# A fused attention and mixture-of-experts kernel: the down product in plain fp32, and fewer waits between scattered adds

## The chip, the cores and the metric

The kernel runs on one core of a Trainium2 chip. The metric is the device time of one execution in microseconds (us), given as the median of several runs. The engines of the core are named as the profile names them: PE (TensorE matmuls; PEld its weight loads), DVE (VectorE), ACT (ScalarE), POOL (GpSimd) and SP (SyncE, which only starts transfers here). Each runs its own instructions in order and waits on semaphores for the others.

## The reference, cut to what matters

Two transformer layers follow each other on x of 32 x 256 x 128 fp32. Each is an attention (16 heads of width 8; kind A over 256 positions with a relative bias, kind B over the batch) and then the same feed-forward layer: one shared expert for every token, and two of seven routed experts, chosen by a router and weighted.

```python
def _expert(h, g, u, d):
    return jnp.einsum('...i,hi->...h', jax.nn.silu(h @ g.T) * (h @ u.T), d)
...
shared_out = _expert(x, sg, su, sd)          # inner width 352
logits = x @ wr.T + rb
probs = jax.nn.softmax(logits, axis=-1)
scores, idx = jax.lax.top_k(probs, 2)
scores = scores / scores.sum(axis=-1, keepdims=True)
...
for e in range(7):
    out = out + w[..., e:e + 1] * _expert(x, rg[e], ru[e], rd[e])
...
x = x + attn_a(layernorm(x)); x = x + ffn(layernorm(x))
x = x + attn_b(layernorm(x)); x = x + ffn(layernorm(x))
```

## The kernel before

**Stages.** After a setup there are four stages: passes A, blocks A, passes B, blocks B. A pass handles 512 tokens: their attention, the router, the shared expert, and a scatter of each token's row to the regions of its two experts in a buffer in DRAM (`sent`, 8 indirect DMAs of POOL, step `place`). Passes overlap: the attention of one pass is interleaved with the expert part of the pass before. There are 16 passes of each kind.

**The planner.** The order of a pass's steps on each engine is not written by hand. `order` merges the attention steps and the expert steps of an engine from lists of needs (`needs_attention`, `needs_experts`) and modelled costs (`WORK`); of the steps that can start earliest it takes the one with the longest chain behind it (kind A) or that of the part further behind (kind B). In the order that it gives for kind B, PE's steps `down1`, `down2` and `end0` of the expert part stand after `bturn` and `bout`, the last attention steps, and are followed by `turn1`, `qk`, `v` and `spread` of the next pass. On POOL the steps stand as `tally`, `cut0`, `place`, `cut1`, `cut2`. On DVE `end0` stands after the last part of `norm2`.

**Blocks.** A block is 512 rows of one routed expert. The number of blocks is fixed, NB = 38 in each stage; a table made from the counts says where each block's rows lie and which expert's weights it takes. Blocks past the last expert are void: they read a spare region, and all add into the same dummy rows. For each block:
- SP loads the rows `xs` (a ring of 4 buffers; the load of block b waits until the adds of block b-4 have landed), then the gate and up weights `w_gu`, then the down weights `w_dn` (rings of 2).
- PE turns the rows (`turn_x`, four transposes into bank T). The turned rows are split into a high part in fp32r and the rest (`xbh`, `xbl`), and each product is three fp32r matmuls: high x high, high x low, low x high (`product`).
- The inner width of 352 is three tiles (n = 0, 1, 2) of 128, 128 and 96. For each: `gate`, `up`, tanh on ACT, two instructions on DVE that make `hid`; then ACT rounds `hid` to `hid_hi` (`high_part`), and POOL (n = 0) or DVE (n = 1, 2) subtracts to get `hid_lo` (`block_low`). `down` is three fp32r matmuls of `hid_hi`, `hid_lo` and the split down weights.
- ACT copies the sum (`block_sum`), PE turns it back (`turn_y`), ACT weights the rows (`weigh`, four instructions writing `yo`), and POOL adds them to the output with four indirect DMAs that accumulate (`add_up`).

PE's body for block b, in its order: gate 0, up 0, turn_x of b+1, gate 1, down 1 of b-1, up 1, down 2 of b-1, gate 2, turn_y of b-1, up 2, down 0. So a block is turned in one body and turned back two bodies later. The add of a block waits for `yo`, and for the adds of the block before to land, whatever their experts. In POOL's body `block_low(b, 0)` stands ahead of `add_up(b-1)`.

In the passes the shared expert's step `cut` does the same split, on ACT and POOL (on ACT and DVE where no attention runs beside). In the setup POOL splits gate, up and down weights of all eight experts, and SP stores those of the seven routed ones in `w_split` (1088 KB each).

## Time and profile before

| | us |
|---|---|
| median of 3 runs | 3122.54 (3102.72 to 3148.47) |
| the profiled execution | 3107.12 |
| its span | 3105.3 |
| setup and passes A | to about 1180 |
| blocks A | about 1180 to 1602 |
| passes B | about 1602 to 2675 |
| blocks B | about 2675 to 3103 |

The trace is that of one execution, and 2 us lie around its span. Busy shares of the span: PE 78%, DVE 62%, ACT 49%, POOL 36%. They are means over four stages of two quite different sorts. Matmuls overlap, so the start of one to the start of the next says more than the duration of one.

### The profile page before, as it was taken

To read this page: it belongs to the slowest core of one execution; us is meant where nothing else is said; L and a number is where in the kernel's file an instruction comes from. 1 tells how busy PE (TensorE), PEld (TensorE's weight loads), DVE (VectorE), ACT (ScalarE), POOL (GpSimd) and SP (SyncE) were. 2 spreads that over 40 slices of the span, in tenths; PEclk is the share of its full clock that TensorE was granted. 3 is DMA by queue.
4 is the path that set the end of the run, shared out by engine and by line. 5 is a ranking of instruction groups with operands and counts; after the bars stand their busy time and mean duration, and the time that the engine had idled before them with its cause. 6 is when DMAs were issued, how large, how long until landed. Compare 5 with 4: busy or idle time off the path is not lost. (4 is left out here: it accounts for less than half of the span.)

```text
span 3105.3 us, 78315 instructions
## 1 busy us (share of the span) xinstructions
PE 2431.4 (78%) x27178; PEld 1690.4 (54%) x27178; DVE 1914.6 (62%) x6390; ACT 1514.0 (49%) x3185; POOL 1103.1 (36%) x1115
## 2 busy tenths in 40 slices
PE   7898988989898875777756877778677788577775
PEld 4566656656665654555534555555455555355554
DVE  4677777777777765777744444444454444477775
ACT  5777777778787763555531222222122222255554
POOL 4322112122211224777640322123221122377777
PEclk8788888888898888999975555555555555799998
DMA  5100000000000005666630000000000000366665
GB/s 172 62 16 18 19 16 20 15 16 15 22 19 16 15 19 159 155 158 156 151 63 6 23 16 22 16 16 21 18 22 16 17 20 16 116 161 155 157 154 103
DMA packets 128145, 184.86 MB, mean 60 GB/s; under 512 B 16128, under 2 KB 90368, under 8 KB 126896
## 3 DMA queue, kind: packets, MB, share of 16 engines
q1 hardware_dynamic: 58160, 134.38, 13.6%
q0 software_dynamic: 51968, 37.26, 8.2%
q10 hardware_dynamic: 17664, 8.39, 1.0%
q8 instruction: 236, 3.87, 0.5%
q14 instruction: 117, 0.96, 0.1%
HBM read 122.47 MB, written 57.50 MB: 58 GB/s over the span
## 5 line engine op out<-in xcount | busy, mean ns | idle before, releaser
L996 ACT ACTIVATE z<-z,nm 128x256 f32<-128x256 f32 x1024 | 440.9, 500 | 107.5 <-DVE nm L1233 105.2
L1233 DVE CUSTOM_DVE_ANT_0 z<-bank_S,big 128x256 f32<-128x256 f32 x1024 | 380.9, 420 | 166.2 <-PE bank_S L1484 124.2
L891 POOL DMA_INDIRECT sent<-rows,slots x256 | 250.2, 977 | 197.0 <-DVE slots L1309 123.0
L954 POOL DMA_INDIRECT x<-yo,xs x152 | 239.9, 1579 | 114.4 <-DMA x<-yo,xs 58.9
L954 POOL DMA_INDIRECT out_x<-yo,xs x152 | 240.4, 1581 | 113.0 <-DMA out_x<-yo,xs 59.9
L720 DVE TENSOR_TENSOR hid_lo<-both,hid_hi 128x512 fp32r<-128x512 f32 (+1 forms) x152 | 210.7, 1386 | 108.6 <-ACT hid_hi L1064 108.6
L1484 PE MATMUL bank_S<-kx,qx 32*128 32x256 f32 x1024 | 227.4, 369 | 54.3 <-issue 34.3
L712 POOL TENSOR_TENSOR hid_lo<-both,hid_hi 128x512 fp32r<-128x512 f32 (+1 forms) x90 | 114.2, 1277 | 374.2 <-ACT hid_hi L1039 373.7
L1064 ACT ACTIVATE hid_hi<-both 128x512 fp32r<-128x512 f32 (+1 forms) x228 | 143.3, 629 | 192.1 <-DVE both L1391 192.1
L1484 PEld LDWEIGHTS bank_S<-kx,qx 32*128 32x128 f32 x1024 | 138.3, 212 | 147.7 <-issue 107.7
L858 POOL COPY h1F<-h 128x512 f32<-128x512 f32 x32 | 19.6, 611 | 476.4 <-DVE h L1252 262.2
L1549 PEld LDWEIGHTS bank_O<-vx,probT 32*32 32x32 f32 x8192 | 125.0, 147 | 112.7 <-issue 110.7
L1549 PE MATMUL bank_O<-vx,probT 32*32 32x9 f32 x8192 | 135.3, 197 | 64.6 <-DVE probT L1267 37.3
L1493 PE MATMUL bank_T<-cst,z 128*128 128x128 f32 x1024 | 179.3, 303 | 6.8 <-ACT probT L705 6.8
L1493 PE MATMUL bank_E<-cst,z 128*128 128x128 f32 x1024 | 180.5, 304 | 0.0
L876 POOL COPY seen<-seen 128x8 f32<-128x8 f32 x32 | 6.1, 191 | 488.6 <-DVE picked L1200 470.5
L705 ACT COPY probT<-bank_T 128x512 f32<-128x512 f32 x256 | 147.0, 574 | 46.7 <-PE bank_T L1493 46.7
L1386 DVE SCALAR_TENSOR_TENSOR both<-both,bank_E 128x512 f32<-128x512 f32 (+1 forms) x228 | 154.4, 677 | 23.2 <-ACT both L1057 22.9
L705 ACT COPY probT<-bank_E 128x512 f32<-128x512 f32 x256 | 150.7, 588 | 36.5 <-PE bank_E L1493 35.8
L1643 PE MATMUL bank_T<-cst,xs 128*128 128x128 f32 x304 | 51.5, 294 | 141.3 <-DMA xs<-sent 98.8
L720 POOL TENSOR_TENSOR hid_lo<-both,hid_hi 128x512 fp32r<-128x512 f32 x76 | 140.0, 1842 | 61.4 <-issue 49.8
L1493 PEld LDWEIGHTS bank_T<-cst,z 128*128 128x128 f32 x1024 | 130.4, 155 | 48.7 <-issue 32.6
(205 smaller groups left out, 5937.7 us busy)
## 6 DMA issues: line engine op xcount, KB each, us to landing
w_ring<-w_split SPq DMA_DIRECT2D x76, 704.0 KB, 4.3
w_ring<-w_split SPq DMA_DIRECT2D x76, 384.0 KB, 3.2
xs<-sent SPq DMA_DIRECT2D x76, 264.0 KB, 2.7
w_split<-w_ring SPq DMA_DIRECT2D x7, 1088.0 KB, 5.0
both<-in_w_raw SPq DMA_DIRECT2D x8, 544.0 KB, 6.0
xin<-in_x SPq DMA_DIRECT2D x16, 256.0 KB, 2.9
sent<-rows,slots POOLq DMA_INDIRECT x256
x<-xo ACTq DMA_DIRECT2D x16, 256.0 KB, 2.3
```

The lines of the kernel that those rows point to most:

```text
L705: copy(probT[:, n % PT_RING, :], turn_bank(n)[:, :]).then_inc(emptied["T"], 1)
L712: eng.tensor_tensor(hid_lo[0:m, n % CUT_RING, :], hid[0:m, n % H_RING, :], hid_hi[0:m, n % CUT_RING, :].bitcast(F32), ALU.subtract).then_i ...
L720: eng.tensor_tensor(hid_lo[0:m, n, :], hid[0:m, n, :], hid_hi[0:m, n, :].bitcast(F32), ALU.subtract).then_inc(blo_ready[n], 1)
L891: pool.indirect_dma_start(out=sent, out_offset=bass.IndirectOffsetOnAxis(ap=slots[:, n:n + 1], axis=0), in_=rows[:, k, t, :], in_offset=No ...
L954: pool.indirect_dma_start(out=summed_in[kind], out_offset=bass.IndirectOffsetOnAxis(ap=xs_int[:, blk.four, t, COL_ID:COL_ID + 1], axis=0), ...
L996: last = act.activation(zt, zt, ACT.Exp, bias=nm[:, n % NM_RING, t:t + 1], scale=-1.0)
L1064: act.activation(hid_hi[0:m, n, :], hid[0:m, n, :], ACT.Copy).then_inc(bhi_ready, 1)
L1233: last = dve.tensor_tensor_reduce(z[:, n % Z_RING, t * SEQ:(t + 1) * SEQ], bank[s][:, t * SEQ:(t + 1) * SEQ], bias_a[:, h, P - P * t:P - P ...
L1386: dve.scalar_tensor_tensor(out=a, in0=a, scalar=1.0, in1=in_blocks(q)[0:m, :], op0=ALU.add, op1=ALU.mult).then_inc(ba_ready, 1)
L1484: last = pe.matmul(bank[s][:, t * SEQ:(t + 1) * SEQ], qx[rows, p.two, g, lo:lo + P], kx[rows, p.two, g, b * SEQ:(b + 1) * SEQ], start=True ...
L1493: last = pe.transpose(turn_bank(n)[:, c:c + P], z[:, n % Z_RING, t * SEQ + k * P:t * SEQ + (k + 1) * P], ident)
L1549: last = pe.matmul(bank["O"][r, h * VW:(h + 1) * VW], probT[r, h % 4, c:c + 32], vx[r, p.two, t, h * VW:(h + 1) * VW], start=True, stop=Tr ...
```

## The change

1. The down product is one fp32 matmul for each tile of the inner width, from `hid` and unsplit down weights (halved once in the setup). In blocks and passes alike `high_part`, `block_low` and `cut` go, with `hid_hi` and `hid_lo`; `down` waits for `hid` alone. The gate and up products stay three fp32r matmuls.
2. The split weights shrink from 1088 to 896 KB per expert, in two transfers; `w_dn` of a block from 384 to 192 KB. In the setup POOL has two instructions fewer per expert.
3. In the blocks PE's `down 2` moves ahead of `up 1`. ACT copies the turned rows straight from bank T to `xbh` (no `xf`, no cast on DVE), and DVE makes `xbl` from bank T.
4. The adds have two semaphores by the parity of the block. Four more DVE instructions put a fourth row into the table: the count that the adds of block b wait for. From the fifth body on POOL loads this count into a register (`value_load`) and waits for it: at a block with another expert than the one before, and at void blocks, for the adds of block b-1; else only for those of b-3. The first bodies wait as before.
5. The planner's list of steps loses `cut`, and `down` costs 0.9 instead of 0.7, so the orders of the passes are planned anew.

```diff
 def needs_experts(eng, step, n):
...
     if step == "down":
-        return [(low, "cut", n)] + ([] if n else [("dve", "rank", 0)])
+        return [("dve", "up", n)] + ([] if n else [("dve", "rank", 0)])
...
     for i in range(FT):
-        out += [("gate", i), ("up", i), ("cut", i), ("down", i)]
+        out += [("gate", i), ("up", i), ("down", i)]
...
-    def sums(self, n):
-        return self.i * (LOOPED * 16 * TOK) + 16 * TOK * (self.half * NB + self.k + n)
+    def sums(self):
+        j = self.k % 2
+        return self.i * (LOOPED // 2 * ADDS) + (self.k // 2 + 1 + self.half * ((NB - j + 1) // 2)) * ADDS
...
     # setup, POOL, expert e
-                pool.tensor_scalar(r[:, 2 * INNER:RAW], r[:, 2 * INNER:RAW], 0.5, None, ALU.mult).then_inc(halved, 1)
-                pool.tensor_copy(dst[:, GU:GU + DN], r[:, 2 * INNER:RAW]).then_inc(high_cut, 1)
-                pool.tensor_tensor(dst[:, GU + DN:WROW], r[:, 2 * INNER:RAW], dst[:, GU:GU + DN].bitcast(F32),
-                                   ALU.subtract).then_inc(weights_cut, 1)
+                pool.tensor_scalar(dn, r[:, 2 * INNER:RAW], 0.5, None, ALU.mult).then_inc(weights_cut, 1)
...
     # blocks, SP
                     if blk.has_before(X_RING - 1):
-                        sp.wait_ge(added, blk.sums(1 - X_RING))
+                        sp.wait_ge(added[blk.two], blk.step(-X_RING).sums())
...
     # blocks, POOL
                 def body(blk, where):
-                    block_low(pool, blk, 0)
                     if where != "first":
-                        add_up(blk.step(-1))
+                        add_up(blk.step(-1), where == "early")
...
+                def add_up(blk, early):
+                    last = blk.step(-1)
+                    if not early:
+                        others = pool.value_load(table[0:1, 3, bass.ds(blk.b, 1)], min_val=ADDS,
+                                                 max_val=ADDS * NB)
+                        pool.wait_ge(added[last.two], others)
+                        alone(pool)
+                    elif blk.has_before(0):
+                        pool.wait_ge(added[last.two], last.sums())
                     pool.wait_ge(by_ready, blk.count(1, 1))
-                    if blk.has_before(0):
-                        pool.wait_ge(added, blk.sums(0))
...
     # blocks, ACT
                 def block_x(blk):
                     act.wait_ge(bx_turned, blk.count(1, 1))
-                    act.wait_ge(bxl_ready, blk.count(1, 0))
-                    act.activation(xf[:, :], bank["T"][:, :], ACT.Copy).then_inc(bxf_ready, 1)
+                    act.wait_ge(bup_done, blk.count(FT, -FT))
+                    act.activation(xbh[:, blk.two, :], bank["T"][:, :], ACT.Copy).then_inc(bxh_ready, 1)
...
                     tanh(blk, 1)
-                    high_part(blk, 0)
-                    high_part(blk, 1)
                     if where != "first":
                         block_sum(blk.step(-1))
                     tanh(blk, 2)
                     if where != "first":
                         weigh(blk.step(-1))
-                    high_part(blk, 2)
...
     # the table, DVE
+                then(dve.tensor_tensor(due[:, 0, 1:NB], whose[:, 1:NB], whose[:, 0:NB - 1], ALU.is_gt))
+                then(dve.scalar_tensor_tensor(out=due[:, 0, 1:NB], in0=whose[:, 1:NB], scalar=float(ROUTED), in1=due[:, 0, 1:NB],
+                                              op0=ALU.is_ge, op1=ALU.max))
+                then(dve.tensor_tensor(due[:, 1, 1:NB], due[:, 0, 1:NB], cst[0:1, C_TURN + 1:C_TURN + NB], ALU.add))
+                dve.tensor_scalar(table[:, 3, 1:NB], due[:, 1, 1:NB], float(k * NB // 2), ADDS, ALU.add, ALU.mult)
...
     # blocks, DVE
-                    dve.tensor_copy(xbh[:, blk.two, :], xf[:, :]).then_inc(bxh_ready, 1)
                     dve.wait_ge(bxh_ready, blk.count(1, 1))
-                    dve.tensor_tensor(xbl[:, blk.two, :], xf[:, :], xbh[:, blk.two, :].bitcast(F32), ALU.subtract
+                    dve.tensor_tensor(xbl[:, blk.two, :], bank["T"][:, :], xbh[:, blk.two, :].bitcast(F32), ALU.subtract
                                       ).then_inc(bxl_ready, 1)
...
                     product_of(blk, 1)
-                    block_low(dve, blk, 1)
                     product_of(blk, 2)
-                    block_low(dve, blk, 2)
...
     # blocks, PE (in the passes alike)
-                    pe.wait_ge(blo_ready[n], blk.count(1, 1))
-                    product(down_bank(blk)[:, :], w_dn[0:m, blk.two, lo:lo + P], w_dn[0:m, blk.two, DN + lo:DN + lo + P],
-                            hid_hi[0:m, n, :], hid_lo[0:m, n, :], start=(n == 0), stop=(n == FT - 1)
-                            ).then_inc(bdown_done, 1)
+                    pe.wait_ge(bh_ready, blk.count(FT, n + 1))
+                    pe.matmul(down_bank(blk)[:, :], w_dn[0:m, blk.two, n * P:(n + 1) * P], hid[0:m, n, :],
+                              start=(n == 0), stop=(n == FT - 1)).then_inc(bdown_done, 1)
...
                     gate(blk, 1)
                     if late:
                         down(late, 1)
+                        down(late, 2)
                     up(blk, 1)
-                    if late:
-                        down(late, 2)
                     gate(blk, 2)
```

## Rows read from the trace of the kernel before

**Rows 1.** Busy time by stage: window, length, each engine, granted clock, DMA share, GB/s

```profile
100.00:1180.00 1080.00, 943.25 (x6282) 638.51 (x6280) 780.73 (x3714) 796.85 (x1749) 234.13 (x332) 0.85 0.06 20
...
1750.00:2660.00 910.00, 704.55 (x15626) 505.08 (x15625) 424.14 (x1455) 202.82 (x349) 217.79 (x300) 0.55 0.07 18
...
2700.00:3105.00 405.00, 291.52 (x1277) 205.55 (x1276) 287.08 (x364) 205.85 (x444) 288.70 (x190) 0.96 0.63 145
```

**Rows 2.** Timeline of POOL in the blocks: start, length, instruction, idle before it and releaser

```profile
1204.93 1.64 POOL L954 DMA_INDIRECT x<-yo,xs  x1 [4.04 <-ACT yo L1077]
...
1404.92 1.56 POOL L954 DMA_INDIRECT x<-yo,xs  x1 [1.80 <-DMA x<-yo,xs]
...
1410.51 1.55 POOL L954 DMA_INDIRECT x<-yo,xs  x1 [0.30 <-issue]
1411.50 1.88 POOL L720 TENSOR_TENSOR hid_lo<-both,hid_hi 128x512 fp32r<-128x512 f32 x1
1415.34 1.56 POOL L954 DMA_INDIRECT x<-yo,xs  x1 [1.97 <-DMA x<-yo,xs]
...
1595.49 1.55 POOL L954 DMA_INDIRECT x<-yo,xs  x1 [2.46 <-issue]
```

**Rows 3.** Timeline of SP's queue: two issues of block 1 and 2, and an xs load later

```profile
1184.71 0.33 SPq L812 DMA_DIRECT2D w_ring<-w_split  x1
1186.54 0.33 SPq L802 DMA_DIRECT2D xs<-sent  x1
...
1414.77 0.33 SPq L802 DMA_DIRECT2D xs<-sent  x1
```

**Rows 4.** Timeline of PE in the same block

```profile
1407.16 0.66 PE L1643 MATMUL bank_T<-cst,xs 128*128 128x128 f32 x4 [1.55 <-DMA xs<-sent]
...
1408.35 0.39 PE L1567 MATMUL bank_Y<-hid_hi,w_ring 128*128 128x512 f32 x1
...
1409.05 0.39 PE L1567 MATMUL bank_E<-xbh,w_ring 128*128 128x512 f32 x1
...
1412.43 0.65 PE L1679 MATMUL bank_O<-cst,total 128*128 128x128 f32 x4 [1.12 <-ACT total L1069]
...
1417.58 0.66 PE L1643 MATMUL bank_T<-cst,xs 128*128 128x128 f32 x4 [1.71 <-DMA xs<-sent]
```

**Rows 5.** Timeline of ACT: the last yo of block 0, and sum and yo around 1412

```profile
1203.73 0.38 ACT L1077 ACTIVATE yo<-bank_O,xs 128x128 f32<-128x128 f32 x1
...
1411.72 0.58 ACT L1069 ACTIVATE total<-bank_Y 128x512 f32<-128x512 f32 x1
...
1413.20 1.15 ACT L1077 ACTIVATE yo<-bank_O,xs 128x128 f32<-128x128 f32 x4 [0.42 <-PE bank_O L1679]
```

**Rows 6.** Timeline of PE: fp32 matmuls over 512 columns (L1456) in either clock

```profile
447.59 1.12 PE L1456 MATMUL bank_E<-xnT,proj 128*128 128x512 f32 x2
448.55 0.38 PE L1514 MATMUL bank_O<-cst,oT 128*128 128x128 f32 x2
...
2059.34 3.78 PE L1456 MATMUL bank_E<-xnT,proj 128*128 128x512 f32 x4 [1.56 <-ACT xnT L980]
2062.91 1.59 PE L1471 MATMUL bank_Y<-proj_vo,xnT 128*128 128x128 f32 x8
```

**Rows 7.** Timeline of PE at the end of a pass of kind B

```profile
2048.40 2.07 PE L1561 MATMUL bank_S<-proj_vo,big 128*128 128x128 f32 x8 [0.76 <-ACT big L1007]
2050.12 0.77 PE L1567 MATMUL bank_Y<-hid_hi,w_here 128*128 128x512 f32 x1
...
2053.72 1.11 PE L1624 MATMUL bank_Y<-cst,total 128*128 128x128 f32 x4 [0.69 <-ACT total L1044]
2056.66 1.11 PE L1427 MATMUL bank_Y<-cst,xn 128*128 128x128 f32 x4 [1.83 <-DVE xo L1341]
```

**Rows 8.** Timeline of POOL: the first pass's h1F, and the lows of a pass B

```profile
107.27 0.61 POOL L858 COPY h1F<-h 128x512 f32<-128x512 f32 x1 [7.95 <-DVE h L1252]
...
2043.46 2.49 POOL L712 TENSOR_TENSOR hid_lo<-both,hid_hi 128x512 fp32r<-128x512 f32 x2
```

More of the change, by code:

```diff
@@ L155 @@
     "gate": {"pe": 0.7, "act": 0.5, "dve": 0.6}, "up": {"pe": 0.7, "dve": 0.6},
[L156 to L157 removed]
+    "down": {"pe": 0.9}, "sum": {"act": 0.5}, "end": {"pe": 0.5, "dve": 0.6, "act": 0.1},
 }
@@ L477, in run_blocks @@
     for k in range(1, LOOPED + 1):
-        body(Blk(kind, 0, k), "middle")
+        body(Blk(kind, 0, k), "early" if k <= 3 else "middle")
     with engine.Fori(0, (NB - 2) // LOOPED - 1) as i:
@@ L1033, in experts @@
                                    ).then_inc(th_ready, 1)
-                elif step == "cut":
-                    m = high(n)
-                    act.wait_ge(h_ready, p.count(same(FT), n + 1))
-                    act.wait_ge(down_done, p.count(same(FT), n + 1 - CUT_RING))
-                    act.activation(hid_hi[0:m, n, :], hid[0:m, n, :], ACT.Copy).then_inc(hh_ready, 1)
                 elif step == "sum":
```

150 lines of the change are left out of this document (59 added, 91 removed).

## The prediction

> **What bounds the kernel now.** I read the stages first [rows 1]: in passes A and B PE is busy for 87% and 77% of the time, in passes B at a granted clock of 0.55, that is mostly at the lower of its two levels (1.2 GHz). In blocks B PE, DVE and POOL all stand near 72%, the clock is at 2.4 GHz nearly throughout, and none is full. So the blocks are held by a chain, and their timelines show which.
>
> POOL first [rows 2]. The four adds of a block are issued 1.86 us apart (1404.92 to 1410.51, three steps). The first add of the next block starts at 1415.34, after waiting for the last to land: a period of 10.42 us, which holds whatever the engines do. The subtraction at 1411.50 lies inside that wait. Over the stage the first add of the first block starts at 1204.93 and that of the last at 1595.49, so 37 periods take 390.6 us: 10.56 each on the mean.
>
> Then the second loop, which is easy to miss. SP loads the rows of a block only when the adds of the block four earlier have landed. PE waits for these rows at every block (1407.16 and 1417.58, idle 1.55 and 1.71 us) [rows 4]. Follow one round:
> - turn_x at 1407.16 to the turn_y at 1412.43: 5.27 us [rows 4]. This turn_y belongs to the block turned two bodies before.
> - turn_y to the end of its yo, at 1413.20 + 1.15: 1.92 us [rows 5].
> - yo to the first add, at 1415.34: 0.99 us [rows 2]. Where POOL was not waiting for its own adds, it took 0.82 (last yo ends at 1204.11, add at 1204.93) [rows 2, 5].
> - first add to the xs load that waits for these adds: 9.85 us (1404.92 to 1414.77) [rows 2, 3].
> - xs load to its turn_x: 2.81 us (1414.77 to 1417.58) [rows 3, 4].
>
> The sum is 20.84 us. It brings us from the turn_x of one block to that of the block two later, so it fills two periods of 10.42. Its slack is the 0.99 - 0.82 = 0.17 us at the third step. The two loops are within 0.1 us per block of each other.
>
> **Blocks: the wait that goes.** Within one expert POOL no longer waits for the block before. Its own loop then is four issues, 7.44 us, and the load of a register. The second loop stays, for SP's wait for block b-4 is unchanged. What it becomes:
> - turn_x to turn_y. PE sat idle for 1.12 us before turn_y, because ACT's sum came late, behind a `hid_hi` [rows 4, 5]. In the new order both downs stand two products further ahead and nothing of ACT's splitting is before the sum, so I drop this idle time. Between lie two downs, each now one fp32 matmul. A down of three fp32r matmuls took 0.70 us (1408.35 to 1409.05) [rows 4]; an fp32 matmul over the same 512 columns takes 0.96 at most at 2.4 GHz (447.59 to 448.55, which may hold a short wait; bounds 0.83 to 0.96) [rows 6]. I take 0.90, near the middle, so 0.4 us for both. 5.27 - 1.12 + 0.40 = 4.55.
> - turn_y to yo stays at 1.92, since tanh 2 stands before it as now.
> - 0.82 to the add (that is where the slack of 0.17 goes), then 9.85 and 2.81 as now. The w_dn transfer halves, but it is issued well before the xs load, so I give nothing for it.
>
> The sum is 19.95 us, or 9.97 per block. That is 0.45 less than 10.42. Over 74 periods in two stages that is 33 us.
>
> New experts still wait for the block before, 10.42 after its first add. There are at most 6 such turns and 2 or 3 void blocks per stage, each late by up to 0.45: I give back 3 us. Blocks: -30.
>
> **The register load.** The trace has none on POOL. SP loads two for each block: from one issue to the next with nothing to wait for, it took 1.83 us, with 0.33 of issue (1184.71 to 1186.54) [rows 3], so 0.75 each at most. POOL will have 9.97 - 7.44 = 2.5 us of idle time per block and loads before `yo` is there, so this costs nothing up to 2.5 us. Bounds: 0, and what a load of over 2.5 us would take. The Trainium skill (DMA: Bandwidth & Descriptors, "Latency and other measured facts") gives a floor of about 600 ns for such a load; by it the sum would be the same.
>
> **PE in the blocks.** 18 fp32r matmuls of gate and up at 0.70 / 3 = 0.233, three downs of 0.90 and two times four transposes of at most 0.66 [rows 4]: 4.2 + 2.7 + 1.3 = 8.2 us. So PE is no bound at 9.97, but is next. DVE loses two subtractions and a cast, ACT three roundings; both were below the period.
>
> Against the change speaks what fp32 costs on PE. The rows say 0.90 for one against 0.70 for three of fp32r. The Trainium skill (FP8 and Floating Point Precision) has four passes for true fp32; by four passes of a 0.233 us matmul a down takes 0.93 us and the sum of the blocks is 1 us worse. What decides is where PE is full, which is the passes.
>
> **Passes B.** A low-clock fp32 matmul takes 1.79 us (four instructions, two to a matmul, 2059.34 to 2062.91) [rows 6]. A split down takes 1.46 (two of them from 2050.12 to 2053.03, the end of what precedes the 0.69 idle) [rows 7]. Three downs cost 3 x 0.33, about 1.0 us, per pass.
> What comes back is order. Today down 1 and down 2 wait for subtractions that POOL does only at 2043.46, after eight scatters [rows 8]; the planner charges 10 us for `place`, so it puts them behind `bout`. Then PE waits 0.69 for the sum and 1.83 for DVE's `xo`, which DVE does after the last norm2 step [rows 7]. Without the cut, down 1 is ready when DVE has `hid`, in the middle of the value products. By the planner's rule (earliest start) I expect both downs in the gaps where PE waits for the attention (0.76 before 2048.40 is one [rows 7]) and `end` before or early in norm2. That saves between 0 and 0.69 + 1.83 + 2 x 0.75 = 4.0 us per pass. I take 2.4, so 1.4 net, for 16 passes: -22. Its bounds are +16 (the old order) and -48.
>
> **Passes A.** PE is at 87% and at 2.4 GHz most of the time [rows 1]; three downs cost 3 x 0.20 = 0.6 us a pass, 9 in all. ACT loses three roundings of 0.63 and is at 74%. It waits for others, so I give that 5. Passes A: +4, bounds -15 and +12.
>
> **Ends and setup.** In the last experts of each kind and at both ends of the blocks the split stood on the path: ACT 0.63, a subtraction and two hand-overs, about 1.8 us at each of four places, less 1 us of table work per stage: -5. The setup gets 11 us shorter on POOL, but POOL then waited 7.95 us for the first attention anyway (107.27) [rows 8]: zero.
>
> **Sum.** -30 - 22 + 4 - 5 = -53. The profiled execution took 3107.1, so it would be 3054; the median of the three runs is 15 us above it, so I predict 3069 for the median.
>
> **The rivals.**
> 1. *PE becomes the bound of the blocks, or the passes gain all they can.* If adds land early enough for the second loop to fall to PE's 8.2 us, rounded up to 8.5 for its waits, 74 periods of 10.56 save 2.06 each: 152 us in place of 30. Against: 9.85 and 2.81 are transfers that the change doesn't touch. Milder, with the whole 4.0 - 1.0 us of each pass B (48) and 0.3 us more per block (30 + 22): 101 with the +4 and -5. These give 3122 - 152 - 22 + 4 - 5 = 2947 to 3021. Chance 0.25.
> 2. *The gain goes to the fp32 matmul.* The planner keeps the tail of pass B and passes A gain nothing: +16 and +9 [rows 6, 7]. In the blocks ACT's sum still comes as late after turn_x, so the 1.12 us stay: 5.27 + 0.40 + 1.92 + 0.82 + 9.85 + 2.81 = 21.07, or 10.53 per block, +8 in 74. With -5 for the ends that is 3150; with the passes alone gone this way it is 3122 - 30 + 25 - 5 = 3112. For it: in passes B PE runs at the low clock and is the fullest engine. Against: nothing that made the sum late is left. Chance 0.2.
> 3. *POOL's register load takes the place of the wait (slower).* The load stands in POOL's queue behind four DMA issues and before the wait for `yo`; the four adds are queued behind it. If it waits until all descriptors are written, and with address arithmetic takes over 3 us, POOL's loop passes 10.42. At 4.5 us it is 11.9: +1.4 x 74 = 104, less 23 from the rest: 3203. It decides from 3.0 us on. Against: SP's 0.75, and the subtraction at 1411.50 that starts 0.99 us after a DMA issue. Chance 0.05.
> 4. *It doesn't do what it says:* every block waits as before because the table's fourth row always says so. The period stays 10.42 and the rest gives 23: 3099. The formula adds one only where the expert rises or is void, so this has hardly a chance of its own; it lies inside the range.
>
> **How the numbers follow.** Forecast 0.5, with its own range 3035 to 3105; rivals 0.25, 0.2 and 0.05. The range takes in most of the first rival and the second: 2985 to 3135. With three runs between 3102 and 3148 a difference of 2% (to 3060) is what can be told. Faster by that: the first rival, and 0.17 of the forecast's 0.5: 0.42. Slower by it: 0.04. The rest is 0.54.
>
> **What the new profile would show.** First adds about 10.0 us apart, with POOL idle before them until `yo`, not a DMA. PE still waiting for xs before turn_x, by about 1.7 us, and not before turn_y. xs loads 9.9 us after the first add of four blocks earlier. In passes B downs 1 and 2 ahead of L1561's `bout` and no 1.83 before `turn1`. Down matmuls of 0.9 us apart at the high clock and 1.8 at the low. I would be wrong if `turn_x` stops waiting (then the second loop is not what I think), if a first add follows a register load, or if the granted clock moves in passes B: at the high level the whole stage would be worth far more than any of these terms.

## The result and the profile after

The changed kernel took 2966.7 us (median of 4 runs, 2962.7 to 2971.6), the kernel before 3131.6 on the same chip (3102.7 to 3148.5): a ratio of 0.948, 95% interval 0.941 to 0.956. That is 5.2% faster. I had forecast 3069 and a range from 2985 to 3135, so the result lies below the range, by 18 us. In a second comparison (run e10 below) the ratio was 0.954 (0.948 to 0.959).

From the page of the kernel after: busy time by engine, the granted clock in 40 slices, the two groups of adds, and the loads of down weights.

```profile
PE 2392.9 (81%) x26854; PEld 1597.4 (54%) x26854; DVE 1664.2 (56%) x6164; ACT 1352.2 (46%) x2861; POOL 867.1 (29%) x934
...
PEclk8898988888898997999985566655665665799998
...
L932 POOL DMA_INDIRECT x<-yo,xs x152 | 237.1, 1560 | 183.0 <-ACT yo L1043 127.2
L932 POOL DMA_INDIRECT out_x<-yo,xs x152 | 236.1, 1553 | 182.5 <-ACT yo L1043 128.6
...
w_dn<-w_split SPq DMA_DIRECT2D x76, 192.0 KB, 2.4
```

POOL now waits before its adds for ACT's `yo`, not for its own adds. To place the gain I cut both traces at the same marks: the starts of the first and the 16th `h1F` copy on POOL (each pass has one) bound the passes, the first adds of the first and the last block bound the blocks. In us:

| | setup | passes A | to blocks | blocks A | to passes | passes B | to blocks | blocks B | end | span |
|---|---|---|---|---|---|---|---|---|---|---|
| before | 107.3 | 1036.3 | 61.4 | 390.6 | 78.1 | 968.7 | 63.1 | 389.1 | 10.9 | 3105.3 |
| after | 102.2 | 1013.4 | 57.3 | 378.3 | 75.2 | 891.8 | 55.3 | 378.3 | 10.8 | 2962.7 |
| predicted change | 0 | +4 | | -15 | | -22 | | -15 | | -53 |
| measured change | -5 | -23 | -4 | -12 | -3 | -77 | -8 | -11 | 0 | -143 |

The change predicted for all the ends together was -5; it was -15.

**The blocks.** POOL in the blocks of the kernel after (answers to [rows 2]), the first adds of four blocks and one second add (1400.81):

```profile
1388.28 1.56 POOL L932 DMA_INDIRECT x<-yo,xs  x1 [2.62 <-DMA x<-yo,xs]
...
1398.94 1.56 POOL L932 DMA_INDIRECT x<-yo,xs  x1 [3.51 <-ACT yo L1043]
1400.81 1.56 POOL L932 DMA_INDIRECT x<-yo,xs  x1 [0.31 <-issue]
...
1407.67 1.56 POOL L932 DMA_INDIRECT x<-yo,xs  x1 [1.58 <-ACT yo L1043]
...
1419.36 1.56 POOL L932 DMA_INDIRECT x<-yo,xs  x1 [4.53 <-ACT yo L1043]
```

SP (answers to [rows 3]), three loads of rows and, before the last, one of down weights:

```profile
1397.94 0.34 SPq L778 DMA_DIRECT2D xs<-sent  x1
...
1407.99 0.33 SPq L778 DMA_DIRECT2D xs<-sent  x1
...
1415.71 0.33 SPq L788 DMA_DIRECT2D w_dn<-w_split  x1
1417.84 0.33 SPq L778 DMA_DIRECT2D xs<-sent  x1
```

PE (answers to [rows 4]), two blocks: `turn_x` is L1604, `turn_y` L1638, the fp32 downs L1630:

```profile
1400.77 0.66 PE L1604 MATMUL bank_T<-cst,xs 128*128 128x128 f32 x4 [0.93 <-DMA xs<-sent]
...
1401.97 1.88 PE L1630 MATMUL bank_S<-both,w_dn 128*128 128x512 f32 x4
1403.28 0.79 PE L1528 MATMUL bank_S<-xbh,w_gu 128*128 128x512 f32 x1
1404.38 0.39 PE L1528 MATMUL bank_E<-xbh,w_gu 128*96 128x512 f32 x1
1405.07 0.60 PE L1638 MATMUL bank_O<-cst,total 128*128 128x128 f32 x4
...
1410.77 1.07 PE L1604 MATMUL bank_T<-cst,xs 128*128 128x128 f32 x4 [2.15 <-DMA xs<-sent]
...
1412.92 2.56 PE L1630 MATMUL bank_Y<-both,w_dn 128*128 128x512 f32 x4
...
1416.70 0.60 PE L1638 MATMUL bank_O<-cst,total 128*128 128x128 f32 x4
```

And ACT's `yo` in that second block (answers to [rows 5]):

```profile
1417.41 1.14 ACT L1043 ACTIVATE yo<-bank_O,xs 128x128 f32<-128x128 f32 x4
```

The reader can follow the ring loop in two interleaved chains. One: add 1398.94, xs load 1407.99 (9.05), turn_x 1410.77 (2.78), turn_y 1416.70 (5.93), end of yo 1418.55 (1.85), add 1419.36 (0.81). That is 20.42 us for two blocks. The other: add 1388.28, load 1397.94 (9.66), turn_x 1400.77 (2.83), turn_y 1405.07 (4.30), add 1407.67 (2.60): 19.39. This second round is shorter than most of its chain, since the add at 1388.28 had itself waited for a landing (2.62).

Over blocks 4 to 35 of blocks A both chains take 20.5 to 20.6 us a round. The first chain takes, on the mean, 9.11 from the add to the load, 2.82 to turn_x, 5.91 to turn_y, 1.86 to the end of `yo` and 0.80 to the add. The second takes 10.51, 2.78, 4.30, 1.81 and 1.21. In the second the load doesn't wait for the landing alone: after the add at 1407.67 it is issued at 1417.84 (10.17), 2.13 us behind the `w_dn` load that stands before it in SP's queue and waits for PE's last down of an earlier block. So I read it that the first chain sets the period and the second follows it. The first adds come alternately some 8 to 9 and 11 to 12.5 us apart, 10.22 on the mean of 37 in either stage, against 10.56 and 10.52 before.

The chains differ at turn_x to turn_y: 5.93 in the first and 4.30 in the second. In the first, PE had stood idle for 2.15 us before turn_x, and its matmuls then run at the lower clock: four transposes 1.07 in place of 0.66, the four fp32 instructions 2.56 in place of 1.88. The wait before `turn_y` is gone. PE's waits in blocks A before (first fence, 1204 to 1595) and after (1204 to 1582), each in total, times, longest:

```profile
PE bank_T L1643 <- DMA xs<-sent: 49.8, 31, 2.5
PE bank_O L1679 <- ACT total L1069: 33.5, 37, 1.1
```

```profile
PE bank_T L1604 <- DMA xs<-sent: 50.7, 32, 3.1
...
PE bank_O L1638 <- ACT total L1035: 0.7, 1, 0.7
```

**The end of a pass B** on PE after (answers to [rows 7]): downs (L1580), `bturn` (L1388, from big), `bout` (L1522), `end` (L1585), `turn1` (L1388, from xn). `xo` is the pass's result, which DVE makes:

```profile
2026.03 2.07 PE L1580 MATMUL bank_Y<-both,here_dn 128*128 128x512 f32 x2
2031.25 1.05 PE L1388 MATMUL bank_T<-cst,big 128*128 128x128 f32 x4
2032.39 2.08 PE L1580 MATMUL bank_Y<-both,here_dn 96*128 96x512 f32 x2
2034.25 1.91 PE L1522 MATMUL bank_S<-proj_vo,big 128*128 128x128 f32 x8
2035.96 1.06 PE L1585 MATMUL bank_Y<-cst,total 128*128 128x128 f32 x4
2037.89 1.11 PE L1388 MATMUL bank_Y<-cst,xn 128*128 128x128 f32 x4 [0.87 <-DVE xo L1302]
```

All three downs now stand before `bout`, no wait for the sum is left, and the 1.83 us before `turn1` have become 0.87.

### The profile page after: what moved, and what is told of

It reads as the page before. It is cut to its first block, busy times and chain, and to the rows that moved or that the text cites. A ratio compares the mean times of both kernels' runs of the same rounds, so it can differ in the third digit from the quotient of the medians.

```text
span 2962.7 us, 76346 instructions
## 1 busy us (share of the span) xinstructions
PE 2392.9 (81%) x26854; PEld 1597.4 (54%) x26854; DVE 1664.2 (56%) x6164; ACT 1352.2 (46%) x2861; POOL 867.1 (29%) x934
## 4 chain that ended last, share of the span: by engine, by line
PE 60%; issue 12%; DVE 9%; DMA 8%; POOL 4%; ACT 4%; ACTq 1%; POOLq 1%; SPq 0%; DVEq 0%
PE bank_S L1445 5%; PE bank_E L1454 5%; PE bank_T L1454 4%; PE bank_E L1528 4%; PE bank_O L1468 4%; PE bank_O L1510 4%; PE bank_Y L1580 4%; PE bank_Y L1630 3%; DMA xs<-sent 3%; PE bank_E L1529 3%; PE bank_E L1530 3%; PE bank_E L1426 3%; PE bank_E L1417 2%; DMA out_x<-yo,xs 2%; DMA x<-yo,xs 2%
## 5 line engine op out<-in xcount | busy, mean ns | idle before, releaser
L1445 PE MATMUL bank_S<-kx,qx 32*128 32x256 f32 x1024 | 212.0, 369 | 75.8 <-issue 35.0
L1445 PEld LDWEIGHTS bank_S<-kx,qx 32*128 32x128 f32 x1024 | 129.2, 212 | 161.5 <-issue 92.7
L1029 ACT ACTIVATE both<-bank_E 128x512 f32<-128x512 f32 (+1 forms) x228 | 136.0, 597 | 170.0 <-PE bank_E L1530 166.1
L1528 PE MATMUL bank_E<-xbh,w_gu 128*128 128x512 f32 (+1 forms) x342 | 198.7, 581 | 2.9 <-DVE xbl L1342 2.9
L1510 PE MATMUL bank_O<-vx,probT 32*32 32x9 f32 x8192 | 118.4, 188 | 100.2 <-DVE probT L1230 85.1
L1510 PEld LDWEIGHTS bank_O<-vx,probT 32*32 32x32 f32 x8192 | 106.7, 131 | 155.9 <-issue 153.5
L1604 PE MATMUL bank_T<-cst,xs 128*128 128x128 f32 x304 | 57.9, 321 | 152.0 <-DMA xs<-sent 109.2
L1009 ACT ACTIVATE both<-bank_E 128x512 f32<-128x512 f32 (+1 forms) x96 | 57.3, 597 | 269.2 <-PE bank_E L1530 269.2
L1454 PEld LDWEIGHTS bank_E<-cst,z 128*128 128x128 f32 x1024 | 125.2, 152 | 49.1 <-issue 29.1
L1468 PE MATMUL bank_O<-probT,vx 128*32 128x256 f32 x2048 | 143.1, 398 | 5.3 <-ACT probT L691 5.2
```

What stands on the lines that cost most here:

```text
L1029: act.activation(th[0:m, n, :], in_blocks(2 * (3 * blk.k + n))[0:m, :], ACT.Tanh, scale=0.5).then_inc(bth_ready, 1)
L1445: last = pe.matmul(bank[s][:, t * SEQ:(t + 1) * SEQ], qx[rows, p.two, g, lo:lo + P], kx[rows, p.two, g, b * SEQ:(b + 1) * SEQ], start=True ...
L1454: last = pe.transpose(turn_bank(n)[:, c:c + P], z[:, n % Z_RING, t * SEQ + k * P:t * SEQ + (k + 1) * P], ident)
L1468: last = pe.matmul(bank["O"][32 * j:32 * j + 32, 0:SEQ], vx[:, p.two, 2 * b + k, c:c + 32], probT[:, u % PT_RING, k * SEQ:(k + 1) * SEQ], ...
L1510: last = pe.matmul(bank["O"][r, h * VW:(h + 1) * VW], probT[r, h % 4, c:c + 32], vx[r, p.two, t, h * VW:(h + 1) * VW], start=True, stop=Tr ...
L1528: pe.matmul(dst, high_w, high_x, start=start, stop=False)
```

## The experiments

Eighteen kernels ran, in five groups, each group on one chip beside the kernel before. Two groups (e1 to e4, e9 to e12) ran where the kernel before took 3104 and 3109 us. The other three (e5 to e8, e13 to e16, e17 and e18) ran where it took 3324 to 3331: the passes are 13 to 15% longer there, the blocks as long. Neither stage lengths of passes nor ratios may be compared across the two kinds: one code had 0.968 (e12) on the one and 0.976 (e6) on the other, and e3's 0.954 stands against 0.971 for e7, which adds only an idle subtraction and whose blocks are as long. The changed kernel itself ran on the faster kind alone. Where it is needed on the slower one, e7 stands for its passes. Passes of one and the same code differ by up to 17 us a stage between profiles (after: A 1013 and 1000; e3: A 997, B 901).

### Which part of the change gives what (e1, e2, e3, e4)

e1: the planner of before plans with its `cut` steps and old costs; these are then dropped from the lists.

```diff
-    return out
+    return {e: [s for s in steps if s[1] != "cut"] for e, steps in out.items()}
```

> The changed kernel with every step of the passes in the order of the kernel before (its planner, with the cuts left out afterwards). Theory 1, the gain in the passes came from the new order, since downs and end no longer stand behind the scatters: the stage of passes B (first to last h1F) goes back from 892 to 940 or more, passes A from 1013 to about 1030 to 1045, the whole to 3030 to 3060. Theory 2, it came from the operations themselves (no cuts, the fp32 matmul keeping PE's clock up): passes B stay at 892 and the whole at 2967, both within 10.

Measured: ratio 0.971 (0.962 to 0.979). Neither theory holds as written. Passes A 1035.3, as before; passes B 921.8, 47 less than before and 30 more than after; blocks 374.5 and 373.1. So in this run passes A gain nothing without the new order, and passes B gain in part.

e2: six row buffers and a loop body of six blocks, in place of four.

```diff
-LOOPED = 4
-X_RING = 4
+LOOPED = 6
+X_RING = 6
```

> The changed kernel with six buffers for the rows of a block in place of four (and a loop of six blocks). Theory 1, the load that waits for the adds of four blocks earlier closes the loop that sets the period of the blocks: with six it opens, first adds come 8.3 to 8.8 apart (PE full) and 10.4 at a new expert or a void block, on the mean about 9.0 in place of 10.22; the whole 2967 - 90 = about 2877. Theory 2, PE's clock or the transfers set the period: the mean stays at 9.9 or more and the whole above 2940.

Measured: ratio 0.916 (0.910 to 0.922), 2839.4 us, 127 less than the changed kernel, and 117 less than e3 on the same chip. Blocks 318.8 and 314.2: a mean period of 8.62 and 8.49. POOL around a new expert, and PE's `turn_x` and a row by window (length, then busy PE, PEld, DVE, ACT, POOL, clock, DMA share, GB/s), all of e2:

```profile
1385.57 1.56 POOL L932 DMA_INDIRECT x<-yo,xs  x1 [0.30 <-issue]
1387.44 1.56 POOL L932 DMA_INDIRECT x<-yo,xs  x1 [0.30 <-issue]
1392.15 1.56 POOL L932 DMA_INDIRECT x<-yo,xs  x1 [3.15 <-DMA x<-yo,xs]
```

```profile
1379.19 0.66 PE L1604 MATMUL bank_T<-cst,xs 128*128 128x128 f32 x4 [0.42 <-DMA xs<-sent]
...
1387.40 0.66 PE L1604 MATMUL bank_T<-cst,xs 128*128 128x128 f32 x4 [0.36 <-DMA xs<-sent]
```

```profile
1372.00:1388.00 16.00, 15.22 (x64) 9.78 (x63) 9.21 (x14) 7.68 (x18) 13.26 (x10) 1.00 0.79 170
```

At a new expert POOL waits (3.15). Behind it, it catches up with blocks 7.45 us apart: four issues of 1.86 and nothing between them, the register load of each block included. In this stretch PE comes to `turn_x` every 8.2 us and is 95% busy. From the fifth block of the stage on it comes every 8.44 us on the mean, and over blocks A it is 89% busy (283.5 of 318.8), with 19.6 us of waits for rows. So PE nearly bounds the blocks now, and a part of the period is still lost where adds must wait.

e3: every block waits for the one before, with the changed kernel's ring of 4. e4: the same with the ring of 6.

```diff
-then(dve.tensor_tensor(due[:, 0, 1:NB], whose[:, 1:NB], whose[:, 0:NB - 1], ALU.is_gt))
+then(dve.tensor_tensor(due[:, 0, 1:NB], whose[:, 1:NB], whose[:, 0:NB - 1], ALU.is_ge))
```

> The changed kernel, but the table makes every block wait for the adds of the block before. Theory 1, the wait that was removed was worth only the few tenths by which it exceeded the ring's loop: period 10.45 to 10.55 in place of 10.22, the whole 2984 to 2992. Theory 2, the wait was worth much and the register load costs most of it back: the period goes to 11 or more and the whole over 3020.

> Six buffers for the rows, and every block waits for the adds of the block before. Theory 1, two loops of nearly the same length: opening one alone gives nothing, the period stays at 10.4 to 10.5, the whole 2980 to 2992, like the run with the wait alone. Theory 2, the ring is all: the period falls below 9.8 and the whole below 2945.

Mean period in blocks A: 10.12 for e3 and 10.49 for e4, ratios 0.954 (0.948 to 0.960) and 0.959 (0.953 to 0.966). With the changed kernel (10.22) and e2 (8.62) this is a table of two by two. Taking away the wait alone gives nothing (10.12 to 10.22), the longer ring alone nothing either, both together 1.5 us a block. Each loop hides the other. Of e3's expectation, theory 1 had the direction right and 10.45 to 10.55 wrong.

e4 is slower than e3 (10.49 to 10.12 a block, in blocks B 10.33 to 10.14), and the traces say where. From the end of the fourth issue to the next add that waits for the landing e4 takes 3.26 us on the mean (63 times), e3 2.73 (46). In e4 the loads wait for the adds of six blocks earlier and run ahead of the adds. Where the 704 KB load of `w_gu` is issued just ahead of the last add, the landing is latest: load at 1255.34, last add at 1255.58, gap 5.51; load at 1414.90, last add at 1416.65, gap 2.87. No run moves this load alone, so that it is the cause isn't shown.

### Why the own loop of the adds got shorter though the wait stayed (e7, e15, e16)

e3 keeps the wait and still is 0.44 us a block below before. On POOL, e3 first, then e15 (described below):

```profile
1417.35 1.56 POOL L932 DMA_INDIRECT x<-yo,xs  x1 [0.30 <-issue]
1421.51 1.56 POOL L932 DMA_INDIRECT x<-yo,xs  x1 [2.60 <-DMA x<-yo,xs]
```

```profile
1411.40 1.56 POOL L933 DMA_INDIRECT x<-yo,xs  x1 [0.30 <-issue]
1416.01 1.56 POOL L933 DMA_INDIRECT x<-yo,xs  x1 [3.05 <-DMA x<-yo,xs]
```

From the end of the fourth issue to the next add where it waited for the landing: 3.14 us on the mean before (65 times), 2.73 in e3 (46). Three suspects: POOL's subtraction, the subtractions on POOL and DVE together, the 384 KB load of down weights.

e7: e3 and an idle subtraction of 128x512 on POOL in each block.

```diff
 def body(blk, where):
+    pool.tensor_tensor(idle_b, idle_a, idle_a, ALU.subtract)
```

> The changed kernel with every block waiting for the adds of the one before, and one more instruction on POOL in every block: a subtraction of two idle 128x512 tiles, where the kernel before has its block_low. Theory 1, this subtraction behind the last add's issue was what made that loop 10.4 us long: its intervals go from 9.75 to 9.85 back to 10.4, the mean from 10.12 to about 10.5, and the whole from 2956 to about 2985. Theory 2, the loop got shorter for another reason (smaller transfers, DVE's instructions with two SBUF inputs): the mean stays within 0.1 of 10.12 and the whole within 10 of 2956.

e16: as e7, and two more such subtractions a block on DVE, before the products of tiles 1 and 2.

```diff
+    idle(blk, 0)
     product_of(blk, 1)
+    idle(blk, 1)
     product_of(blk, 2)
```

> The changed kernel with every block waiting, and with three idle subtractions of 128x512 of two SBUF inputs a block, one on POOL and two on DVE, as the split had them (their results are not used). Rival S: landing gap 3.1 us instead of 2.6, period 10.4 to 10.5, blocks 386. Theory W: period stays at 10.1, blocks 374 to 378; POOL's subtraction takes 1.9 us and DVE's over 2 where they meet.

e15: e3, and each down load takes 384 KB from the same rows; the added half isn't used.

```diff
-sp.dma_start(w_dn[:, blk.two, :], w[:, GU:WROW])
+sp.dma_start(w_wide[:, blk.two, :], w[:, GU - DN:WROW])
```

> The changed kernel with every block waiting, and the 384 KB load of down rows that the kernel before had in each block, instead of 192 KB (the added half is not used). Theory W (the larger load delays the landing of the adds by half a us): from the last add's end to the next 3.1 us instead of 2.6 to 2.7, period 10.4 to 10.5, blocks 12 us a stage longer than in the kernel that waits with the small load (374 to 375): 386. Rival S (it was the subtractions on POOL and DVE together): period stays 10.1, blocks 374 to 377.

Mean landing gap: e7 2.63 (42 times), e16 2.72 (49), e15 3.05 (66). So the subtractions don't delay the landing, and the larger load makes it as late as it was. The period of e15 rose only to 10.24, not to the 10.4 to 10.5 expected, and its blocks to 379 (e7 375 and 378). The load explains the later landing, and about a quarter of the 0.44 us. A further part is in the adds themselves: from the first issue to the end of the fourth they take 7.32 us on the mean before (7.34 in e9), 7.14 in e3 and e15, and 7.22 in e16, where single steps of up to 2.3 us come back with the subtractions. Of before's excess of 0.18 us e16 has 0.08; what makes the rest of it, and the last 0.14 of the period, stays open. The ratios (e7 0.971, e15 0.975, e16 0.969) don't tell the three apart.

### The passes: order or operations (e5, e6, e8, e9 to e14, e17)

e6, and again e12: the kernel before, with the low part cut on DVE in place of POOL. The planner then makes a third order, with the downs early too.

```diff
 def low_engine(with_attention):
-    return "pool" if with_attention else "dve"
+    return "dve"
```

> The kernel before, with the subtraction of the split in the passes on DVE in place of POOL, so that the downs no longer stand behind the scatters and the planner orders them early. Split and three fp32r matmuls stay. Theory 1, the order is the gain of the passes: passes B go from 969 to 920 to 935, passes A (1036) to 1025 or less, the whole to about 3060. Theory 2, only the removal of the split helps, and DVE's three more instructions cost: passes B stay above 955 and passes A rise above 1036.

e5: the changed kernel, the shared expert's down in the passes as one fp32r matmul (the low parts are left out there).

```diff
-pe.matmul(bank["Y"], here_dn[0:m, n * P:(n + 1) * P], hid[0:m, n, :], start=(n == 0),
+pe.matmul(bank["Y"], here_dn[0:m, n * P:(n + 1) * P], hid_r[0:m, n, :], start=(n == 0),
```

> The changed kernel, its order and its other steps unchanged, but the shared expert's down product in the passes is one fp32r matmul of rounded operands in place of one fp32 matmul (it leaves out the low parts of the product). Theory 1, the fp32 matmul is a plain cost on PE: passes B (892 to 901 in the runs so far) lose three times about 1.2 us in each of 16 passes, to 835 to 850, passes A (997 to 1013) lose 25 to 30, the whole is about 2880. Theory 2, the fp32 matmul holds up PE's granted clock in passes B: the clock there falls from 0.59 to 0.61 to 0.56 or less, the stage stays at 885 or more, and the whole at 2930 or more.

e8: e2, and 12 matmuls into a bank nobody reads, before the first value product of each pass B.

```diff
+if n == 0:
+    for _ in range(12):
+        pe.matmul(bank["E2"], here_gu[:, 0:P], xh, start=True, stop=True)
```

> The run with six row buffers, and in each pass of kind B twelve fp32r matmuls over 512 columns into the unused bank E2, ahead of the first value product, where PE waits 5.6 us for the transposed scores. Their result is read by nobody. Theory 1, PE's idle time there is what lets its clock fall in passes B: the granted clock of the stage rises from 0.59 to 0.65 or more, the stage falls from 899 to 870 or less, the whole from 2839 to 2810 or less. Theory 2, the clock is low for the sparse small matmuls and the twelve only fill the wait, or delay what follows: the clock stays, the stage is 899 or up to 20 longer.

e6: ratio 0.976 (0.970 to 0.982) with the split kept. e5: 0.961 (0.957 to 0.965), passes A 1143 and B 1011 against e7's 1150 and 1027: a down that costs next to nothing on PE is worth 7 and 15 us, not the 57 in B that its price at the lower clock would give. In passes B PE's busy time fell by 36 us, the granted clock from 0.58 to 0.56, and its idle time rose by 21. e8: passes B 1028.1 against e7's 1026.5, no gain in time. But the granted clock was 0.62 against 0.58. The twelve matmuls took 64 us in the place of 61 us of waiting for `probT` (the transposed scores); all other work of PE got 21 us shorter, and other idle time 19 longer. So both of e8's theories failed: the clock can be raised so, and the stage isn't shorter for it. From e6 I took it that the order gives all, and asked for one table on one chip.

e9 is the kernel before, e10 the changed one, e11 is e1, e12 is e6:

> The kernel before, profiled on the chip on which its three variants run, so that the four make a table of two by two by stage: order of steps (old or new) against operations (split or fp32). Theory 1 (the passes' gain is the order): passes A and B of this kernel and of the old order with fp32 are both slower than those of the two with the new order, by some 20 us in A and 30 to 50 us in B, whatever the chip. Theory 2 (the fp32 product gives it): passes with fp32 are faster by 40 us in B in either order.

> The changed kernel on the same chip. Theory 1: passes A and B within 10 us of those of the kernel before with the low cut on DVE (new order, split kept). Theory 2: passes B 40 us shorter than there. Both: blocks 10 to 12 us a stage shorter than before's.

> The changed kernel's operations in the step order of before. Theory 1: passes A as before's within 5 us and passes B at most 20 us below before's. Theory 2: passes B 40 us or more below before's, as in the first run of it, where it was 47.

> Before's operations with the low part cut on DVE, which gives the early order of the down steps. Theory 1: passes A 20 us and passes B 30 to 50 us below before's, blocks and gaps as before's: ratio 0.975 to 0.98. Theory 2: passes B within 15 us of before's, since the split is kept: ratio 0.99.

| | order | down | ratio (95%) | passes A | passes B | PE busy in B | clock in B |
|---|---|---|---|---|---|---|---|
| e9 | before | split, POOL | 0.999 (0.995 to 1.003) | 1048.7 | 961.9 | 744.0 | 0.54 |
| e11 | before | fp32 | 0.967 (0.961 to 0.972) | 1033.4 | 923.5 | 731.9 | 0.58 |
| e12 | third | split, DVE | 0.968 (0.961 to 0.974) | 1018.0 | 885.3 | 677.4 | 0.60 |
| e10 | after | fp32 | 0.954 (0.948 to 0.959) | 1000.4 | 892.4 | 687.4 | 0.61 |

e12 changes two things, though: the engine and, through it, the order. So three more. e13: before's operations (cut on POOL) in the changed kernel's order, written out. e14: the changed kernel's fp32 in e12's order, planned as in e1 but for a cut on DVE. e17: before's order written out, the cut on DVE.

```diff
+WRITTEN = {"pe": [...], "dve": [...], "act": [...], "pool": [...]}
+BESIDE["B"].update(WRITTEN)
```

```diff
-    low = "pool" if attention else "dve"
+    low = "dve"
```

> The kernel before, with its split, cuts on ACT and POOL kept, in the changed kernel's order of steps beside the attention (the three cut steps put right behind what they need). Theory 1 (the passes' gain is the order alone): passes A near 1005 us and passes B near 890 to 900, as in the changed kernel; blocks as before's; in all 2995 to 3010. Theory 2 (fp32 is what makes the early down steps pay, since down need not wait for copy and subtraction): passes B 920 or more, in all above 3025.

> The changed kernel with its fp32 products, in the order of the run with the low cut on DVE. Against that run only the passes' operations differ. Theory 1: passes within 10 us of it (A 1018, B 885), the rest as the changed kernel: 2950 to 2970. Theory 2 (fp32 gives 20 us a stage in any order): A under 1000 and B under 870: 2920 to 2935.

> The kernel before with its own order of steps beside the attention (A and B) and the low cut of the passes moved from POOL to DVE, put right behind the copy that it needs. Theory E (the engine of the cut, out of POOL's queue and off its contention, is what the run with the cut on DVE gained): ratio to before 0.97 to 0.98, nearly all of that run's 3.2 per cent. Theory J (order and a short way to the down product are needed jointly; in the old order the down steps stand so late that their operand is ready anyway): ratio 0.99 to 1.01, passes within 20 us a stage of before's.

| (the slower kind of chip) | order | down | ratio (95%) | passes A | passes B |
|---|---|---|---|---|---|
| e17 | before | split, DVE | 1.008 (1.004 to 1.011) | 1162.1 | 1098.2 |
| e13 | after | split, POOL | 0.999 (0.997 to 1.001) | 1149.7 | 1076.9 |
| e6 | third | split, DVE | 0.976 (0.970 to 0.982) | 1148.2 | 1007.7 |
| e7 | after | fp32 | 0.971 (0.966 to 0.975) | 1149.6 | 1026.5 |
| e14 | third | fp32 | 0.956 (0.951 to 0.960) | 1123.5 | 989.3 |

My theory that the order alone gives it fell with e13: the new order with the old operations is worth nothing (POOL's second and third low parts still stand behind the eight scatters). The engine of the cut alone gives nothing either (e17). The operations alone gave 38 us of passes B in e11. The rest of the gain in passes B needs an early down and an operand that is there in time. In passes A the runs don't agree on the operations: with the changed kernel's order fp32 gives nothing (e13 and e7), with the third order 25 us (e6 and e14). PE's waits in passes B of e13 show what stands in the way, a row that e7, with the same order, doesn't have:

```profile
PE bank_Y L1574 <- POOL hid_lo L719: 29.8, 16, 2.2
```

Of the 50 us between e13 and e7 in passes B, PE waited 30 for POOL's low parts and was busy 7 longer (750.3 and 742.9); the rest is in other waits.

### A version that beats both (e18)

e18 is e14 with the ring of 6.

> The changed kernel with six row buffers (and six blocks to a loop turn) and the order of steps of the run with the low cut on DVE. The two gains lie in different stages and should add: 0.9156 to before for the ring alone, and some 2 per cent more from the order (A 25, B 35 us shorter than the changed kernel's on one chip): ratio 0.895 to 0.905 theory 1. Rival: the order's gain was noise of the passes, which vary by 15 us a stage between profiles: ratio 0.91 to 0.92.

Measured on a slower chip: ratio 0.923 (0.920 to 0.925). That lies just outside both ranges. e8, whose ring is the same and whose order is the changed kernel's (its twelve extra matmuls left passes B as long as e7's), had 0.939 (0.935 to 0.943) on another chip of this kind, so the order adds 1.7%. On the faster kind only e2 ran, with 0.916, and I reckoned my 0.895 to 0.905 from there: that e2 gained 265 us there, while e8 gains 201 here, is what I had left out.

## Why the prediction was wrong

**The step that failed is passes B**, the term of -22 (order -2.4, fp32 +1.0 a pass), measured -77, and -70 between e9 and e10. The sign and the move were right: the planner did put both downs ahead of `bout`, and the wait for the sum went. But I priced only the idle time at the end of a pass. On one chip (e9, e10), passes B lost 12.9 us of PE's idle time (217.9 to 205.0) and 56.6 of its busy time. The groups of PE in passes B, before (e9) first, then after (e10), count, busy, mean ns:

```profile
L1549 PE MATMUL bank_O<-vx,probT 32*32 32x9 f32 x7680 | 126.9, 197 | 54.7 <-DVE probT L1267 32.1 <-issue 21.0 <-DVE big L1273 0.9
...
L1456 PE MATMUL bank_E<-xnT,proj 128*128 128x512 f32 x56 | 52.9, 1101 | 22.4 <-ACT xnT L980 22.4
...
L1567 PE MATMUL bank_E<-xh,w_here 128*128 128x512 f32 x60 | 47.4, 791 | 0.0
...
L1561 PE MATMUL bank_S<-proj_vo,big 128*128 128x128 f32 x120 | 31.1, 441 | 11.4 <-ACT big L1007 11.4
```

```profile
L1510 PE MATMUL bank_O<-vx,probT 32*32 32x9 f32 x7680 | 110.8, 188 | 93.2 <-DVE probT L1230 79.8 <-issue 10.1 <-DVE big L1236 0.7
...
L1528 PE MATMUL bank_E<-xh,here_gu 128*128 128x512 f32 x60 | 44.5, 742 | 0.3
L1417 PE MATMUL bank_E<-xnT,proj 128*128 128x512 f32 x56 | 41.7, 886 | 26.7 <-ACT xnT L957 26.7
...
L1522 PE MATMUL bank_S<-proj_vo,big 128*128 128x128 f32 x120 | 24.5, 372 | 2.6 <-ACT big L984 2.6
```

The same instructions in the same number got shorter: the value products by 16.1 us, the fp32 projections by 11.2, `bout` by 6.6, and so on. Nothing was taken from them; more of them ran at the higher clock (0.54 before, 0.61 after). The waits behind `probT` even grew, from 32 to 80 us, and the stage is shorter all the same. Both parts of the change have a share in it: the clock was 0.58 with fp32 in the old order (e11). The downs themselves went from 85.4 to 78.0 busy, where I had added 16: at one and the same clock an fp32 down costs more, as I said, but more of them fell where the clock is high.

I had named this as what would make me wrong ("if the granted clock moves in passes B") and given it no chance and no price, though [rows 1] had it at 0.55, near the 0.50 of the lower level, so that there was far more room above than below.

**Passes A**, +4 predicted (bounds -15 to +12), was -23, and -48 between e9 and e10. With the old order and fp32, e1 and e11 had 1 and 15 us of these, the rest came only with the new order. I had priced no gain of order in passes A at all. PE's busy time fell there too (937.6 to 892.7), with the granted clock at 0.85 and 0.88.

**Blocks**, -30 predicted, was -23, and that the number came near is in part luck. Right was that the ring loop stays and sets the period, that POOL waits for `yo`, and PE for xs and no longer before `turn_y`. Wrong was the step that gave the gain to the wait that goes. With the wait kept (e3) the blocks are as short, 374 and 375 in place of 378, since the loop of the adds no longer takes the 10.42 us that I had called fixed "whatever the engines do": where POOL waits for a landing, the first adds of e3 come 9.87 us apart, those of before 10.49.

In the ring loop the mis-sized term is turn_x to turn_y. I had 4.55; in the chain that sets the period it is 5.91, as the clock falls in every second block after a wait of 2 to 3 us, and in the other 4.30. Against it went the first add to the load, 9.11 in place of 9.85. Together with the small terms that is 20.5 in place of 19.95. The statement that the halved w_dn transfer gives nothing was wrong: it brings the landing of the adds forward by 0.3 to 0.4 us (e15), and SP's load of rows waits for this landing too, so it is in the ring loop as well. From the first add to that load e3 takes 9.26 on the mean and e15 9.46; by my estimate from these that is 0.1 us a block.

**The price of an fp32 down** at the high clock was right: from 1401.97 two of them and a product of three take until 1404.38; less the 0.70 of the product this is 0.86 each (I took 0.90). At the low clock 2032.39 to 2034.25 is 1.86 (1.79). The Trainium skill (FP8 and Floating Point Precision, "TensorE Precision Notes") has four passes for true fp32; my estimate from that and the rows, 0.93, is a little above the 0.86 measured. (The 1 us that I gave for the difference was a slip: 0.03 a block in 74 is about 2. It is in no sum.)

**The register load** was hidden, as forecast: in e2 POOL's blocks follow each other at 7.45 us with 0.30 between all issues. Rival 3 fell. The 600 ns that the Trainium skill gives for such a load (DMA: Bandwidth & Descriptors, "Latency and other measured facts") can be neither seen nor refuted in that row, as nothing waits for it.

**PE next at 8.2 us** was right: e2 reaches 8.2 from turn_x to turn_x at 95% busy, 8.44 on the mean. Rival 1, which had the blocks fall to 8.5, didn't happen in the changed kernel, and does as soon as the ring is longer. Its range (2947 to 3021) does hold the 2967, but by luck: its milder form had 48 us for passes B from idle time, and they gave 70 to 77, most of it busy time. Rival 2 had ACT's sum stay late; the 33.5 us before `turn_y` are gone.

**The ends**, -5 predicted, were -15 at four places, and the setup -5 in place of 0.

## What to carry to other kernels

When two loops of nearly equal length hold a stage, opening one shows almost nothing; price the other first, and open both (here a wait and two row buffers: 10.12 us a block with neither opened, 10.22 and 10.49 with one, 8.62 with both). When a stage runs at the lower of PE's clocks, a change of order isn't priced by the idle time it removes alone: look at what the mean durations of untouched instructions would be at the higher clock, and give that case a chance. An order that uses an operand early is worth nothing while the operand comes late, so test order and operations apart, on one chip, before crediting either.

## What the runs showed of the hardware

**The granted clock in passes B differs between the kernels.** One pass in slices of 4 us, during the value products, before (e9), then after (e10); the columns as in [rows 1]:

```profile
2164.59:2168.59 4.00, 4.00 (x134) 3.30 (x126) 2.08 (x8) 0.63 (x1) 1.55 (x3) 0.50 0.01 4
2168.59:2172.59 4.00, 4.00 (x134) 3.40 (x134) 1.24 (x3) 0.63 (x1) 2.93 (x3) 0.50 0.11 38
2172.59:2176.59 4.00, 4.00 (x134) 2.84 (x132) 1.24 (x3) 0.59 (x1) 2.94 (x4) 0.50 0.17 55
```

```profile
2005.84:2009.84 4.00, 4.00 (x135) 3.69 (x133) 2.24 (x8) 0.00 (x0) 0.54 (x2) 0.50 0.02 4
2009.84:2013.84 4.00, 3.90 (x134) 2.28 (x133) 0.69 (x1) 0.60 (x1) 3.09 (x4) 0.78 0.17 54
2013.84:2017.84 4.00, 3.80 (x136) 2.34 (x134) 2.25 (x6) 0.59 (x1) 3.08 (x4) 1.00 0.18 55
```

PE is busy throughout in the first three slices and 1.2 GHz is granted in all of them; in the other trace it is as busy in the first slice, and then 2.4 GHz is granted, in a part of the second slice and all of the third. Both stretches mix value products with products of 512 columns, but not the same ones: after, one of them is an fp32 down (2010.08), before, a down of three fp32r matmuls (2170.69). Which property brings the clock up I can't say. The fp32 product alone isn't it: with the split kept, the third order has 0.60 (e12), and fp32 in the old order 0.58 (e11), against 0.54, while the new order with the old operations has 0.55 (e13, on the slower kind). Twelve more matmuls at the start of that stretch raised the stage's clock (0.58 in e7, 0.62 in e8) and gained no time. That the clock rose from before to after is shown, what raises it stays open.

**Four accumulating adds** let the next add start 2.6 to 2.7 us after the end of the last issue on the mean in e3, e7 and e16, and 3.05 in e15, where a load of 384 KB in place of 192 KB runs beside them. With small down loads but six row buffers (e4) it is 3.26, up to 5.5.

**Chips differ.** The same kernel before took 3104 to 3109 us in two groups and 3324 to 3331 in the others. By stage, in e12 and e6, which are one code, the passes took 253 us more and the blocks 3 less. In passes B, from e3 to e7 (125 us), 88 us are idle time of PE before value products for which the profile shows no releaser (11.0 and 98.8), and 42 are busy time. The gains differ with it: e3 takes 148 us off the kernel before on the one kind, and e7 94 on the other. Without the kernel before in every group, the comparison of e1 with e6 would have been worthless, and even the ratios shift by one to two points between the kinds (e12 and e6, e3 and e7).
